# A transformer layer on one core: the order of the matmuls at a head boundary, and the first microseconds

## The reference

```
qkv  = x @ w_qkv + b_qkv;   q, k = rope(q), rope(k)      per head
out  = softmax(q k^T / sqrt(16)) v;   a = out @ w_out + b_out
x1   = layernorm(x + a)
y    = (silu(x1 @ wg^T) * (x1 @ wu^T)) @ wd^T            wg, wu, wd: integers / 127, hidden 768
out  = layernorm(x1 + y)
```

## Time and profile before

| | us |
|---|---|
| median of 3 runs | 2866.97 (2866.47 to 2878.27) |
| the profiled execution | 2870.14 |
| its span, first to last instruction | 2868.1 |
| PE busy in the span | 2811.7 (98%) |
| DVE busy | 2702.9 (94%) |
| ACT busy | 2591.9 (90%) |
| POOL busy | 1416.7 (49%) |
| mean granted TensorE clock | 0.989 |

### The profile page before, as it was taken

The page is one execution under the profiler, slowest core; times in us unless marked ns, Lnnn a source line. Parts: engine busy times, 40 slices in busy tenths (PEclk is TensorE's granted clock), DMA queues, the critical chain, the costliest instruction groups (busy, mean ns, idle before and its releaser), DMA issues. The chain is left out here.

```text
span 2868.1 us, 70575 instructions
## 1 busy us (share of the span) xinstructions
PE 2811.7 (98%) x27022; PEld 862.5 (30%) x27022; DVE 2702.9 (94%) x3088; ACT 2591.9 (90%) x4778; POOL 1416.7 (49%) x4133
## 2 busy tenths in 40 slices
PE   8989999999999999999999999999999999999998
PEld 4531222222222222222222222222222222246665
DVE  7989999999999999999999999999999999947777
ACT  5756999999999999999999999999999999976555
POOL 7851444444444444444444444444444444436553
PEclk9978999999999999999999999999999999999999
DMA  5431111111111111111111111111111111233431
GB/s 194 142 116 28 36 35 36 35 36 35 35 35 35 34 35 36 35 36 36 35 35 35 36 35 35 35 35 36 35 35 36 35 35 35 70 90 92 118 96 38
DMA packets 121519, 146.56 MB, mean 51 GB/s; under 512 B 52832, under 2 KB 87520, under 8 KB 121180
## 3 DMA queue, kind: packets, MB, share of 16 engines
q1 hardware_dynamic: 120892, 142.02, 17.0%
q10 hardware_dynamic: 288, 0.01, 0.0%
HBM read 106.30 MB, written 35.13 MB: 49 GB/s over the span
## 5 line engine op out<-in xcount | busy, mean ns | idle before, releaser
L102 DVE TENSOR_REDUCE tile_max<-s_ps 128x1 f32<-128x1024 f32 (+1 forms) x2048 | 2282.4, 1185 | 8.8 <-PE s_ps L91 2.8
L1063 ACT ACTIVATE probs<-st_ps 128x512 f32<-128x512 f32 x4096 | 2202.2, 601 | 71.0 <-PE st_ps L942 41.1
L953 PE MATMUL o_ps<-probs,kept_v 128*17 128x256 f32 x16384 | 1283.1, 385 | 25.7 <-ACT sums L1032 25.7
L91 PE MATMUL s_ps<-k,q 64*128 64x512 f16 x4096 | 1266.2, 386 | 11.0 <-DVE tile_max L102 9.2
L942 PE MATMUL st_ps<-q,k 64*128 64x512 f16 x4096 | 1249.5, 382 | 1.1 <-ACT probs L1063 0.8
L1198 POOL TENSOR_TENSOR larger<-spared 128x256 f32<-128x256 f32 x1107 | 342.8, 310 | 675.6 <-ACT spared L1038 598.5
L953 PEld LDWEIGHTS o_ps<-probs,kept_v 128*17 128x17 f32 x16384 | 273.6, 95 | 852.2 <-ACT probs L1063 445.6
L942 PEld LDWEIGHTS st_ps<-q,k 64*128 64x128 f16 x4096 | 256.1, 94 | 902.0 <-ACT probs L1063 842.3
L1207 POOL TENSOR_TENSOR spared<-spared,larger 128x256 f32<-128x256 f32 x984 | 318.4, 324 | 81.9
L1200 POOL TENSOR_SCALAR larger<-larger 128x256 f32<-128x256 f32 x1107 | 261.4, 236 | 96.8
L91 PEld LDWEIGHTS s_ps<-k,q 64*128 64x128 f16 x4096 | 250.2, 94 | 50.4 <-DVE tile_max L102 46.5
(11 more groups left out here) (119 smaller groups left out, 1625.3 us busy)
## 6 DMA issues: line engine op xcount, KB each, us to landing
q<-q_parts SPq DMA_DIRECT2D x193, 128.0 KB
k<-k_parts SPq DMA_DIRECT2D x193, 128.0 KB
x_t<-in_x_t SPq DMA_DIRECT2D x16, 512.0 KB, 7.2
q_parts<-parts SPq DMA_DIRECT2D x32, 256.0 KB, 2.6
k_parts<-parts SPq DMA_DIRECT2D x32, 256.0 KB, 2.6
heads_out<-sums SPq DMA_DIRECT2D x256, 32.0 KB, 2.1
kept_v<-heads_out SPq DMA_DIRECT2D x16, 512.0 KB, 6.1
kept_v<-inverses_out SPq DMA_DIRECT2D x32, 256.0 KB
```

The source lines that it names most:

```text
L91: mm = pe.matmul(s["s_ps"][g % 2][:, j * BANK:(j + 1) * BANK], s["q"][h % 2][rows, r // KW * P:(r // KW + 1) * P], s["k"][h % 2][rows, at: ...
L102: dve.tensor_reduce(s["tile_max"][h % 2][:, r // KW, r % KW:r % KW + 1], s["s_ps"][g % 2][:, columns], AX.X, ALU.max).then_inc(s["s_read"], 1)
L953: mm = pe.matmul(o_ps[c * 32:c * 32 + VM, at:at + HALF], t["kept"][:, h, kt, :], probs[(h * KT + kt) % RING][:, c * BANK + at:c * BANK + a ...
L1063: act.activation(probs[(h * KT + kt) % RING][:, c * BANK:(c + 1) * BANK], st_ps[n % ST][:, :], ACT.Exp, scale=scale).then_inc(exp_done, 1)
```

## The change

Four places differ.

1. At the start, the 512 columns of the q and k weights come in one transfer, ahead of x, and PE waits for all of them. Each of the four chunks of the first batch has its own semaphore; PE's chunks of batch 0 wait for theirs. DVE takes the maxima of the first batch by chunks (`first_x_maxima`: eight reductions of 128x512 into `x_part`, then one small reduction into `x_top`) and the products, all ahead of the first rotation.
2. In PE's rounds, the last two halves of the `times_v` of the head before both stand in round 1; round 2 has none. In rounds 1 and 2 block 2n+1 stands ahead of `times_v`, in the other rounds behind it as before.
3. ACT's copy of the sums stands behind the fourth exponential of the next head.
4. DVE clears its buffers behind tile 16; the addition to the output bias stays behind tile 18.

```diff
-            weights(slice(0, P), first_weights_in)
-            load(0, 0, first_x_in)
-            weights(slice(P, 2 * D), weights_in)
+            weights(slice(0, 2 * D), weights_in)
+            load(0, 0, first_x_in[0])
             tables(slice(0, CH), first_tables_in)
             for c in range(1, NC):
-                load(0, c, x_in[0])
+                load(0, c, first_x_in[c])
...
-                if k == 0:
-                    pe.wait_ge(first_x_in, 16)
-                elif k == 1 or c == 0:
+                if b == 0:
+                    pe.wait_ge(first_x_in[c], 16)
+                elif c == 0:
                     pe.wait_ge(x_in[b % 2], x_landed(b))
...
-                    if k == 0 and m == 1:
-                        pe.wait_ge(weights_in, 16)
...
+            def first_x_maxima():
+                for c in range(NC):
+                    dve.wait_ge(first_x_in[c], 16)
+                    for kd in range(KD):
+                        dve.tensor_reduce(x_part[:, kd, c:c + 1], x_t[0][:, kd, c * CH:(c + 1) * CH], AX.X, ALU.max,
+                                          apply_absolute_value=True).then_inc(part_topped, 1)
+                dve.wait_ge(part_topped, NC * KD)
+                dve.tensor_reduce(x_top[:, :], x_part[:, :, :], AX.X, ALU.max).then_inc(topped, KD)
...
             dve.wait_ge(bias_in, 2 * 16)
+            first_x_maxima()
+            products(0)
             dve.wait_ge(first_tables_in, 2 * 16)
...
                 rope(k, 0)
-                if k == 0:
-                    x_maxima(0)
-                    products(0)
...
-    ODD_LAST = range(EXPS // 2)
+    LAST_V = 1
...
-                    odd_last = h + 1 < HEADS and n in ODD_LAST
+                    odd_last = h + 1 < HEADS and n not in (LAST_V, LAST_V + 1)
                     if not odd_last:
                         scores_t(h, 2 * n + 1)
                     before, half = divmod(n - 3, 2)
                     if before >= 0:
                         times_v(h, before, half)
-                    elif h > 0:
+                    elif h > 0 and n <= LAST_V:
                         times_v(h - 1, KT + before, half)
+                        if n == LAST_V:
+                            times_v(h - 1, KT - 1, 1)
                     if odd_last:
                         scores_t(h, 2 * n + 1)
...
-                    if e == QC and h > 0:
+                    if e == QC - 1 and h > 0:
                         drain(h - 1)
...
                 maximum(g)
+                if g == MAXES // 2:
+                    clear()
                 if g == MAXES // 2 + 2:
-                    clear()
                     dve.wait_ge(bias_done, 1)
```

More of the change, by code:

```diff
@@ L137, in project @@
         x_top = sb("x_top", [P, KD])
+        x_part = sb("x_part", [P, KD, NC])
         bounds = sb("bounds", [P, BOUNDS])
@@ L149, in project @@
         bound_ps = v_ps[1][:, 0, 0:BOUNDS]
-        first_weights_in = sem("first_weights_in")
         weights_in = sem("weights_in")
@@ L156, in project @@
         tables_in = sem("tables_in")
-        first_x_in = sem("first_x_in")
+        first_x_in = [sem(f"first_x_in{c}") for c in range(NC)]
         x_in = [sem(f"x_in{i}") for i in range(2)]
@@ L161, in project @@
         topped = sem("topped_qk")
+        part_topped = sem("part_topped_qk")
         bounded = sem("bounded")
@@ L181, in x_landed @@
         def x_landed(b):
-            return ((b // 2 + 1) * NC - (b % 2 == 0)) * 16
+            return (b // 2 + b % 2) * NC * 16
         block = ctx.enter_context(nc.Block())
@@ L274, in chunk @@
                     mm.then_inc(v_done, 1)
-            pe.wait_ge(first_weights_in, 16)
+            pe.wait_ge(weights_in, 16)
             pe.wait_ge(ones_set, 1)
@@ L350, in _ @@
         def _(dve):
+            def first_x_maxima():
[6 more added lines that the diff above has]
+                dve.tensor_reduce(x_top[:, :], x_part[:, :, :], AX.X, ALU.max).then_inc(topped, KD)
             def x_maxima(b):
                 wait(dve, bounded, BOUNDS * b)
-                if b == 0:
-                    dve.wait_ge(first_x_in, 16)
                 dve.wait_ge(x_in[b % 2], x_landed(b))
@@ L403, in rope @@
                                   ).then_inc(roped_done, 1)
-            dve.wait_ge(first_weights_in, 16)
             dve.wait_ge(weights_in, 16)
```

## The result

| | before | after |
|---|---|---|
| median, us | 2867.61 (2866.30 to 2878.27) | 2872.86 (2871.93 to 2880.03) |
| ratio after / before | | 1.0023, 95% interval 1.0017 to 1.0029 |
| profiled execution, us (span) | 2870.14 (2868.1) | 2872.2 (2870.4) |
| DVE busy | 2702.9 (94%) | 2697.6 (94%) |

The changed kernel takes 5.3 us more in the medians (0.23%): slower, beyond what the timing leaves open, and within the 0.5% that the prediction took as its mark. Eleven of its 20 times lie between 2871.93 and 2872.87 us and nine between 2876.16 and 2880.03, while 17 of the 20 of the kernel before lie between 2866.30 and 2870.12; the medians of the two lower groups are 4.9 us apart.

A forecast was written before the change was run, and what follows sets the result against it. DVE was taken to bound the kernel, PE's order mattering only where it delivers late. Heads +10.5, start -2.0 and clears -0.55 sum to +8.0 us, a median of 2875 us; own range 2870 to 2881, overall 2857 to 2885.

The forecast's parts named there:

- late tile of round 2: Head boundary: PE's new round 1 delays round 2's tile by 0.68 against 0.3 slack, so DVE loses 0.38 us per head.
- drain stall: Round 3: PE's 0.41 us wait for the copy of the sums goes, saving DVE 0.13 us per head.
- given back at the first half: After a head's first half maximum, PE has caught up and DVE gets its tiles sooner: -0.08 us per head.
- start, to the first score matmul: First batch: PE's pause before chunk 1 shrinks and its clock holds, 0.3 + 1.7: -2.0 us, bounds +0.6 and -2.5.
- clears: DVE's buffer clears move into its 1.74 us wait for tile 17: -0.55 us, between -0.6 and 0.
- last head: The last head has no maxima beside it; no effect assumed there, between -0.3 and +0.5 us.
- faster rival: Head boundary: round 2's tile is in time and only the stall's removal counts: 2856 or 2851 us; chance 0.20.
- a reciprocal (0.26): DVE's work per head: the reciprocal was priced at 0.26 us within 35.57 us of own work.
- neutral rival: Heads: DVE's small losses merely change place, so only start and clears count: -2.55, 2864.4 us; chance 0.15.
- PE starts 0.9 late: Start: weights and x both land at about 7.2 us in the new order, so PE starts 0.9 us later than 6.33.
- the prediction's estimate: Start: by a fixed 2.0 us per DMA, one transfer fewer would start PE 1 us early; the prediction held overlap against it.
- the 1.7 for the clock: Start: with the shorter pause chunk 1's 16 matmuls take about 7.0 us instead of 8.81, a gain of 1.7.

The follow-up runs named there:

- order_only: Kernel before with the changed PE order alone and the copy of the sums behind the fourth exponential: 2874.99 us, ratio 1.0022.
- double_paired: Changed kernel with every `st_ps` still beside an `s_ps` and the copy of the sums behind the third exponential: 2859.31 us, ratio 0.9968.
- old_order_copy4: Kernel before with the new start and earlier clears, old PE order, copy of the sums behind the fourth exponential instead of the fifth: 2863.20 us, ratio 0.9984.
- after_copy5: Changed kernel with the copy of the sums back behind the fifth exponential: 2883.76 us in one timing.
- double_paired_copy4: double_paired with the copy of the sums behind the fourth exponential instead of the third: 2870.96 us in one timing.
- weights_only: Kernel before with only the first weights in one transfer, maxima of x where they were: 2874.31 us in one timing.
- before_again: Kernel before, unchanged, timed and profiled again as a kernel of its own: 2869.08 us, ratio 1.000.
- start_only: Kernel before with the new start alone (weights in one transfer, maxima of x by chunks ahead of the rotation): 2867.09 us, ratio 1.0002.

## Why the prediction was right, and where its terms were not

| term | predicted, us | measured |
|---|---|---|
| late tile of round 2 | +0.38 | +0.36 |
| drain stall | -0.13 | -0.13 |
| given back at the first half | -0.08 | -0.13 |
| per head | +0.17 | +0.096 |
| heads together | +10.5 | +5.9 |
| start, to the first score matmul | -2.0 | -2.8 in the profile |
| clears | -0.55 | -0.7 |
| last head | 0 (-0.3 to +0.5) | -0.1 to +0.2 |

The measured column is from the profiles: per head, medians over the heads of DVE's start-to-start steps, less the 1.13 that a maximum costs.

**The late tile: right.** The forecast was a step of about 1.51; it is 1.48, in the changed kernel and in order_only. The slack of 0.3 against the delay of 0.68 decided it as said, and the faster rival fails there. double_paired shows the same threshold from the other side: with the delay 0.24 shorter DVE's step is 0.22 shorter, and the kernel is faster than before. The faster rival was thus one block and one place of the copy away from the change as made.

**The drain stall: right.** It is gone, and it was worth 0.13 on the tile of round 4 (before, the step behind round 3 was 0.124 over and the overshoot 0.010). old_order_copy4 confirms its kind: half the wait on PE, 0.05 us per head.

**What comes back: the sign right, the size wrong.** The term gave 0.08 and it is 0.13, and this is most of the distance between 0.17 and 0.10. The step that failed is "a reciprocal (0.26)" in DVE's own 35.57 us. (The terms as printed there add up to 35.54; with 1.131 for a maximum they give 35.57.) Its price is 0.18, as the changed kernel's 1397.75 to 1397.93 shows; the other 0.08 was DVE waiting for the next tile, with no idle time on record because the reciprocal's own record covered it. DVE's own work is 35.49, the head lost 0.44 and not 0.36, and there was more to give back: 0.08 at the tile behind the reciprocal and 0.04 at the one behind that. That PE's stall in round 3 was the cause of this loss, as the prediction supposed, is shown by after_copy5 and double_paired_copy4: with the stall the 0.26 returns. The neutral rival, losses that only change place, was half right: a third of what the new order costs is taken back elsewhere.

**The start: right in the profile, not in the medians.** "PE starts 0.9 late" failed: x landed as early as before with all the weights ahead of it. The Trainium skill (DMA: Bandwidth & Descriptors, Anatomy of one DMA) gives a DMA that GpSimd issues a fixed cost of about 2.0 us; the prediction's estimate carried this over to SyncE's transfers, and by it PE would start 1 us earlier. The rows show neither: 6.18 and 6.30 with one weights transfer, 6.33 with two, and from 5.77 to 6.66 over all 13 profiles, whichever way the weights come. ACT's copy is late next, as forecast, with a pause of 0.79 (forecast 0.7). Against the profile of the kernel before, the 1.7 for the clock are gained in full (chunk 1 takes 7.11 instead of 8.81). But order_only and weights_only pass the same pause of 1.97 at a granted clock of 1.00, and before_again does not (0.71). An execution that keeps its clock there gains only the rest. The 1.2 us of start_only's seven lower times fit that; how often the clock falls cannot be read from single profiles. The median loses more of it to the upper group of times. This is an argument, not shown, for why the profiles differ by 2.3 us and the medians by 5.3: the profiled execution of the kernel before had lost its clock and is 2.5 us over its median, that of the changed kernel is 0.7 under its own. What is left in the medians is mostly the heads' term, and order_only alone has it.

**The clears: right.** The wait took them in; 0.65 to 0.7 us, where 0.6 was the bound.

**The last head: right.** From the last maximum to the end of the span the two profiles of the new order have 379.74 and 379.70 us, and the six of the old one 379.54 to 379.93, which leaves between -0.1 and +0.2 against the kernel before and the same kernel profiled again. The last two distances between copies are 0.67 longer (80.17 against 79.50), but they begin at a copy that now stands earlier in its head and end at one that stands where it did. Inside the last head PE does wait longer, with no maxima beside it and the doubled `times_v` ahead of `st_ps` (PE after; before, the only wait there was one of 0.21 for the copy), and the end of the span does not show it:

```profile
2511.04 0.39 PE L945 MATMUL st_ps<-q,k 64*128 64x512 f16 x1 [0.54 <-ACT probs L1068]
```

**The sum.** +8.0 was forecast and +5.3 measured; 2875.0 against 2872.86. The heads' term was 4.6 us too high (10.5 against 5.9), mostly because the first half maximum gave back more than was put down (0.13 for 0.08 per head). The start and the clears, forecast at -2.55, are worth about -0.7 in the medians (5.3 less 5.9) and made up for 1.9 of that. The forecast owes some of its closeness to errors of opposite sign.

## What to carry to other kernels

Where one engine has no idle time, take its budget from start-to-start steps, and check the price of each small instruction in it at a place where what follows cannot be late: an instruction that stands where the engine would wait hides the wait in its own step. A reordering on the feeding engine costs only what exceeds the slack at the next delivery, so look for the one piece that can leave that stretch; here it was a 0.24 us block without a partner, and keeping it paired, together with the copy one place earlier, turned +0.2% into -0.3%. The instruction that frees a buffer belongs about where its own wait ends, rather ahead of it than behind (in the two faster kernels ACT waits 0.15 and 0.21 us for it): one place too late cost 0.05 to 0.18 us per head, up to three quarters of it at tiles some eight steps behind the stall. And before two instructions serve as marks for a sum, make sure that the change moved neither of them.

## What the runs showed of the hardware

- A 128x1 `scalar_tensor_tensor` on DVE lasted 0.16 us in the five places where POOL was idle when it started. In the other 47 places it ended 0.01 to 0.02 us behind one of POOL's `tensor_tensor` instructions: 44 times after 1.14 to 1.30 us, three times only behind the fifth in a row, after 7.03 to 7.05. The loads of x do not cause the long wait. Why five pass is open.
- The same pause of 1.97 us on PE, at the same place of the program, was followed by a lower granted clock in two profiles (0.78 and 0.71 over 20 to 24 us, so part of the stretch at 1.2 GHz) and by 1.00 in two others.
- 384 KB more weights ahead of x in one queue did not delay x (6.12 to 6.66 us in ten profiles, against 5.77 to 6.42 in three), while all the weights were there at 4.67 in one transfer and at 7.32 where the second of two stood behind x.
